# A graph kernel with four adjacency layers: masks made four blocks ahead, left-over weights made in the first sweep, and three transfer slots instead of four with one more pair of blocks kept in SBUF

## What is computed

```
layer 0: 1 - 0.1*h - 0.01*sum(h * (adj @ h))
layer 1: twice  h = tanh(concat(adj @ h, h) @ W[k])
layer 2: support = h @ weight
         rank = cumsum(adj != 0, axis=1); deg = rank[:, -1:]; k = min(deg, 100)
         w = (adj != 0) * 0.5 ** (k - (rank - (deg - k)))   where that position is > 0
         out = w @ support + bias
layer 3: tanh(concat(h, t) @ W1 + b1) @ W2 + b2 + adj @ (h @ B.T) - rowsum(adj) * (h @ B.T)
```

## Time and profile before

| what | us |
|---|---|
| median of three runs | 791.98 (788.62 to 795.04) |
| the profiled execution, its own time | 788.66 |
| its span, first to last instruction | 786.6 |

### The profile page before, as it was taken

One profiled execution on the slowest core, in us unless ns is written; L12 is line 12 of the kernel. 1 busy time (PEld: TensorE's weight loads), 2 busy tenths in 40 slices (PEclk: granted clock), 3 DMA queues, 4 the chain that ended last, 5 costly groups with the idle time before them and its releaser, 6 DMA issues.

```text
span 786.6 us, 10295 instructions
## 1 busy us (share of the span) xinstructions
PE 714.9 (91%) x3752; PEld 287.1 (36%) x3752; DVE 468.5 (60%) x789; ACT 182.8 (23%) x279; POOL 168.7 (21%) x172
## 2 busy tenths in 40 slices
PE   1999999999899999999999967888888889999997
PEld 0333333333334333344444432333333333433333
DVE  5677666767988878555566625878888831111111
ACT  2000000000001000001010015777777731111111
POOL 5011110012000000012112232343454414222231
PEclk9999999999999999999999987999999999999999
DMA  9799999999999999999999948888999979999994
GB/s 372 312 423 420 421 419 420 421 418 366 345 387 408 385 383 374 379 358 359 362 370 367 350 192 330 328 309 316 341 349 339 330 247 373 351 369 369 367 367 191
DMA packets 48659, 280.96 MB, mean 357 GB/s; under 512 B 5985, under 2 KB 15329, under 8 KB 15713
## 3 DMA queue, kind: packets, MB, share of 16 engines
q1 hardware_dynamic: 38754, 271.39, 88.6%
q10 hardware_dynamic: 9856, 8.92, 3.5%
HBM read 275.56 MB, written 4.73 MB: 356 GB/s over the span
## 4 chain that ended last, share of the span: by engine, by line
PE 51%; DMA 31%; DVE 8%; POOL 4%; issue 4%; ACT 1%; SPq 0%; ACTq 0%; DVEq 0%; POOLq 0%
PE accA L993 34%; DMA land<-adj_blocks 15%; DMA cache<-adj_blocks 8%; DMA uS<-counts 5%; PE spare L1025 4%; DMA xin<-x_rows 3%; PE accA L1036 3%; DVE uS L835 2%; PE nat L926 2%; PE tr L902 2%; POOL rstd L495 2%; PE spare L1008 1%; PE nat L922 1%; DVE uS L825 1%; PE nat L918 1%
## 5 line engine op out<-in xcount | busy, mean ns | idle before, releaser
L993 PE MATMUL accA<-land,X 128*64 128x512 f32 x1536 | 370.1, 600 | 10.7 <-DMA land<-adj_blocks 7.8
L825 DVE TENSOR_TENSOR uS<-uS,land 128x512 f32<-128x512 f32 x192 | 133.1, 693 | 65.4 <-DMA land<-adj_blocks 56.1
L993 PEld LDWEIGHTS accA<-land,X 128*64 128x64 f32 x1536 | 103.0, 137 | 187.6 <-issue 136.2
L835 DVE TENSOR_SCALAR uS<-land 128x1024 bf16<-128x1024 f32 (+1 forms) x192 | 134.2, 747 | 53.6 <-DMA land<-adj_blocks 52.6
L993 PE MATMUL accA<-cache,X 128*64 128x512 f32 x512 | 126.5, 602 | 15.2 <-DVE X L867 12.5
L502 POOL TENSOR_TENSOR hS<-tS 128x256 f32<-128x256 f32 x32 | 25.6, 802 | 475.5 <-DVE tS L706 475.5
L407 ACT ACTIVATE wS<-spare 128x1024 uint16<-128x1024 f32 x112 | 108.6, 1033 | 56.2 <-PE spare L1025 56.0
L1025 PE MATMUL spare<-uS,triA 128*128 128x512 bf16 x256 | 78.5, 389 | 30.7 <-DMA uS<-counts 11.0
L1036 PE MATMUL accA<-wS,X 128*128 128x512 bf16 x256 | 77.7, 386 | 0.0
L583 ACT ACTIVATE rowsT<-tr 128x256 f32<-128x256 f32 x40 | 15.4, 385 | 236.2 <-PE tr L902 236.2
L993 PEld LDWEIGHTS accA<-cache,X 128*64 128x64 f32 x512 | 36.6, 138 | 83.2 <-issue 76.9
(11 more groups left out here) (78 smaller groups left out, 465.8 us busy)
## 6 DMA issues: line engine op xcount, KB each, us to landing
land<-adj_blocks SPq DMA_DIRECT2D x240, 1024.0 KB, 7.6
cache<-adj_blocks SPq DMA_DIRECT2D x16, 1024.0 KB, 12.3
xin<-x_rows ACTq DMA_DIRECT2D x32, 128.0 KB, 5.5
x_rows<-zS ACTq DMA_DIRECT2D x24, 128.0 KB, 5.0
cache<-x_rows SPq DMA_DIRECT2D x1, 1024.0 KB, 4.9
loadjS<-adj_blocks SPq DMA_DIRECT2D x64, 8.0 KB
uS<-counts SPq DMA_DIRECT2D x64, 4.0 KB
out_rows<-zS ACTq DMA_DIRECT2D x8, 128.0 KB, 7.3
```

The lines of the kernel that those rows point to most:

```text
L825: nc.vector.tensor_tensor(total, total, of[:, i * W:(i + 1) * W], ALU.add)\
L835: nc.vector.tensor_scalar(masks(b)[0:rows, :], block_of(p, c, b)[0:rows, :], 0.0, None, ALU.not_equal)\
L993: last = nc.tensor.matmul(accA[k * D:(k + 1) * D, c % 2, :], tile(X[p % 2], TQ * b + k), of[:, k * W:(k + 1) * W], start=(b == 0), stop=(b ...
```

## The change

The edits, with the names of the new code:

1. `LAND` is 3. `cached_pairs(7)` is (0, 2, 4), so 17 pairs stay in SBUF and 47 are transferred in a sweep after the first.
2. In the first sweep the two pairs of chunk 1 that stay in SBUF are issued ahead of pair (0, 6) (`L0_LOADS`).
3. The left-over weights are made in L0, for each chunk: SP brings the left-over adjacency (`left_adjacency`, from an array that the host lays out), VectorE combines it with the counts, ScalarE forms the weight, and a transfer puts it in DRAM. In L2 one transfer per chunk brings it back (`left_over`). GpSimd's three operations in L2 are gone. The left-over rows are copied chunk by chunk, by four small transfers each (`left_rows_of`), at the head of the steps of L1B from chunk 2 on, and in L2.
4. In L2 the masks are made `LEAD` = 4 blocks ahead of the block to which the other work belongs; `EVAC_LAG` is 1.
5. The row sums of L1B's chunks go ahead of the `nat` matmuls, into a bank of their own use, and TensorE waits for other semaphores at the start of L2.

```diff
 def cached_pairs(c):
-    return (0, 4)
+    return (0, 2, 4) if c == 7 else (0, 4)
...
+L0_LOADS = [(c, k) for c in range(NC) for k in range(PAIRS)]
+for _k in cached_pairs(1):
+    L0_LOADS.remove((1, _k))
+    L0_LOADS.insert(L0_LOADS.index((0, 6)), (1, _k))
+
+LAND = 3
-LAND = 4
...
+LEAD = 4
-EVAC_LAG = 3
+EVAC_LAG = 1
...
-        sums_p = spare[:, 0, 0:4]
+        sums_p = nat[:, CH:CH + 4]
...
+            def left_adjacency(c):
+                if c:
+                    sp.wait_ge(left_later, c)
+                else:
+                    sp.wait_ge(cleared, 1)
+                sp.dma_start(loadjS[1:2 * NT:2, :], left_in_d[:, c * W:(c + 1) * W]).then_inc(left_adj, 16)
             def left_over(c):
-                if c:
-                    sp.wait_ge(left_ready, c)
-                rows = adj_in.rearrange("(b p) (t w) -> p b t w", p=P, t=2 * TQ)
-                for k in range(PAIRS):
-                    sp.dma_start(loadjS[4 * k:4 * k + 4, :], rows[LAST, c * PAIRS + k]).then_inc(left_in, 16)
-                sp.dma_start(locntS[:, :], tile_counts[c, :, 1]).then_inc(left_in, 16)
+                if c >= 2:
+                    sp.wait_ge(weighed, c - 1)
+                sp.dma_start(left_weights(c), left_d[c]).then_inc(left_in[c % 2], 16)
+
+            def left_rows_of(c):
+                sp.wait_ge(cleared, 1)
+                sp.wait_ge(copy_used, copied_no(L1B, c, 1) + 1)
+                for t in range(4 * c, 4 * c + 4):
+                    sp.dma_start(loS[2 * t + 1:2 * t + 2, :], tile16(t)[LAST:P, :]).then_inc(left_rows, 16)
...
-                if g == 6:
-                    sp.wait_ge(copy_used, copied_no(L1B, NC - 1, 1) + 1)
-                    sp.dma_start(left_d, X[1][LAST:P, :].bitcast(F16)).then_inc(left_rows, 16)
-                    sp.wait_ge(left_rows, 16)
-                    sp.dma_start(loS[:, :], left_d.rearrange("o (t w) -> (o t) w", w=2 * D)).then_inc(left_rows, 16)
+                if g in (2, 6):
+                    left_rows_of(NC - 2 if g == 2 else NC - 1)
...
                 if p == L2 and c == 0:
                     sp.wait_ge(counts_out, 16 * NC)
+                    sp.wait_ge(left_out, 16 * NC)
                     left_over(0)
+                    left_over(1)
                     after_masks(0)
-                for k in range(PAIRS):
+                if p == L1B and c >= 2:
+                    left_rows_of(c - 2)
+                if (p, c) == (L1A, 0):
+                    left_adjacency(NC - 1)
+                for c, k in [(c, k) for k in range(PAIRS)] if p != L0 else L0_LOADS[c * PAIRS:(c + 1) * PAIRS]:
...
+                    if p == L0 and k == 5 and c:
+                        left_adjacency(c - 1)
...
+                    nc.scalar.activation(loweightS, lolaterS, ACT.Relu, bias=wt("full", rows=(0, D)),
+                                         scale=-BIT * BIT).then_inc(left_made, 1)
+                    act.wait_ge(left_made, c + 1)
+                    act.dma_start(left_d[c], loweightS).then_inc(left_out, 16)
...
+                        dve.wait_ge(left_adj, 16 * (c + 1))
...
+                        nc.vector.scalar_tensor_tensor(out=lolaterS, in0=loadjS, scalar=0.0, in1=countS,
+                                                       op0=ALU.is_equal, op1=ALU.max).then_inc(left_later, 1)
...
+                if p == L2 and NQ * c + b + LEAD < NQ * NC:
+                    mask(p, (NQ * c + b + LEAD) // NQ, (b + LEAD) % NQ)
...
             def step(p, c, before, before2):
+                if p == L2 and c == 0:
+                    for b in range(LEAD):
+                        mask(p, c, b)
```

More of the change, by code:

```diff
@@ L913, in epilogue @@
                     nat_free(nat_no(p, c, 0))
+                    if p == L1B:
+                        pe.wait_ge(totalled, totalled_no(L1B, c, TOTALS[L1B][-1]))
+                        if c:
+                            pe.wait_ge(rowsum_ready, c)
+                        for j in range(4):
+                            last = nc.tensor.matmul(sums_p[:, j:j + 1], totals(c)[:, j * P:(j + 1) * P], wt("ones"),
+                                                    start=True, stop=True)
+                        last.then_inc(sums_done, 1)
                     if p in (L1A, L1B):
@@ L928, in epilogue @@
                     last.then_inc(nat_done, 1)
-                    if p == L1B:
-                        pe.wait_ge(totalled, totalled_no(L1B, c, TOTALS[L1B][-1]))
-                        if c:
-                            pe.wait_ge(rowsum_ready, c)
-                        for j in range(4):
-                            last = nc.tensor.matmul(sums_p[:, j:j + 1], totals(c)[:, j * P:(j + 1) * P], wt("ones"),
-                                                    start=True, stop=True)
-                        last.then_inc(sums_done, 1)
                 if at == ("transpose" if p == L3 else HT_PE.get(p, None)):
@@ L1052, in step @@
                     count(NC - 1, NQ - 1)
-                if p == L1B and c == 0:
+                if p == L2 and c == 0:
                     pe.wait_ge(count_ready, NC)
-                if p == L2 and c == 0:
-                    pe.wait_ge(rowsum_ready, NC)
                 if s >= 2:
```

84 lines of the change are left out of this document (42 added, 42 removed).

## The result

The changed kernel takes 905.4 us in the median (900.21 to 920.36, four runs), the kernel before 793.5 beside it. The ratio is 1.141, 95% interval 1.131 to 1.151. The prediction was 845, with a range of 816 to 872. The direction and the largest term were right; the size was not.

A forecast was written before the change was run, and what follows sets the result against it. It took transfers to bound L0, TensorE to bound L1A, L1B and L3, and only L2 to have room. 50.4 + 12 + 3 + 2.2 + 3 + 2.4 + 0.5 - 18.3 = 55.2 us more gave 845 us, range 816 to 872.

The forecast's parts named there:

- the largest term: SP's added wait in L1B: TensorE stalls 8.4 us in each of six chunks, 50.4 us.
- L0: start, traffic: L0: queue dry sooner at the start with three slots, 3 us; adjacency in and weights out, 2.2 us.
- L2 with its start: L2: chunks 1.9 us shorter, 13.3 us over seven, plus 5 us at its start; 18.3 us gained.
- three slots in L3: L3: loads issued one pair later cost almost nothing, as chunks are over 1 us longer; 0.5 us.
- The wait at the head of L1B's chunks: L1B, chunks 2 to 7: SP waits for GpSimd's split, holding all loads; TensorE stands 8.4 us each.
- The clock: L1B: each stall lowers TensorE's clock for the work behind it, 2.0 us a stall, 12 us for six.
- the clock stays up: Rival, L1B: stalls do not lower the clock, so 12 us less, 833 us; chance 0.12.
- Three slots: L1A, L1B, L3: loads issued one pair later still land nearly in time; 2.4, 0 and 0.5 us.
- three slots starve the sweeps: Rival: 1.3 us lost in each of 24 chunks of L0, L1A and L3, 31 us, 873 us; chance 0.06.
- The turn to L1A: L0's end: SP waits for VectorE's last work, so L1A's first loads land late; 3 us, bounds 0 and 5.
- the early loads fill no hole: L0: the two pairs moved ahead of (0, 6) stand behind (0, 5), which itself waits for a slot.
- the first half turn: L2 chunk from block 12's move to block 4's: TensorE bounds, 8.9 us; the other half, VectorE-bound, 9.4 us.

The follow-up runs named there:

- e1: The changed kernel with L1B's four left-over row copies and their wait moved behind the chunk's last load: 841.6 us, ratio 1.060 to the kernel before.
- e7: The changed kernel with ten extra unused matmuls put ahead of block 2 in L1B's chunks 2 to 7: 898.4 us, ratio 1.124 to the kernel before.
- e2: The kernel before with only SP's wait for GpSimd's split added at the head of L1B's chunks 2 to 7, no copies: 846.5 us, ratio 1.068.
- e3: The kernel before with LAND = 3 and nothing else: 839.8 us, ratio 1.060.
- e5: The changed kernel with four slots, pairs (0, 4) kept, and L1B's row copies behind the chunk's last load: 787.2 us, ratio 0.989 to the kernel before.
- e4: The changed kernel with LAND = 4 and pairs (0, 4) kept in every chunk: 867.9 us, ratio 1.094 to the kernel before.
- e13: e12 with the xin transfer in L2 issued three blocks earlier in ScalarE's program: 780.7 us, ratio 0.982 to the kernel before.
- e12: e5 with the last left-over adjacency row fetched behind L1A's load (0, 3), not at L1A's head: 787.8 us, ratio 0.988 to the kernel before.
- e8: The kernel before with only L2's masks made four blocks ahead (LEAD 4, EVAC_LAG 1): 791.9 us, ratio 0.993.

## Why the prediction was right and where it failed

In the prediction's own terms, with the span's 117.9 us set beside its 55.2. (Two slips in its sums are small: 8 chunks of 0.31 us of queue are 2.5 and not 2.2, and 843.9 with the 3.3 of the median is 847 and not 845.)

| term | predicted | measured |
|---|---|---|
| L1B: wait, clock, three slots | 50.4 + 12 + 0 = 62.4 | 84.2 |
| L0: start, traffic | 3 + 2.2 = 5.2 | 10.2 |
| turn to L1A, three slots in L1A | 3 + 2.4 = 5.4 | 20.9 |
| L2 with its start | -18.3 | -7.0 |
| three slots in L3 | 0.5 | 9.6 |

1. **The wait at the head of L1B's chunks: right.** Place, chain, number of stalls and releaser are as predicted. With the fourth slot back, moving it is worth 77.5 us of L1B. The stall was 9.4 us and not 8.4, since a small transfer's issue was 0.6 us there and not 0.34; I had taken the duration from another kind of small transfer. Of the 21.8 us by which L1B missed, 5.7 are the wait (e1 gives back 68.1 of L1B for 62.4) and 16.1 what e1's L1B is still longer than before's: the slots.

2. **The clock: right.** 2.0 us a stall was predicted; e7 gives 1.6 of time, e2 2.5 of busy time. The rival "the clock stays up" is refuted by the 0.51 above.

3. **Three slots: this is the step that failed.** It read: "The load issued at 257.08 would go out at 258.8 and, alone, land at 263.7 ... So 0.3 us for a chunk of L1A ... L1B and L3 have chunks over 1 us longer, so 0 and 0.5." It followed one load of one chunk, and took 4.9 us for it, the time of a load into idle queues. With three slots the median was 6.2, with two loads still ahead of it. The ring as a whole should have been summed: with the latency of the very row used (7.05 us) and the 1.89 us of sweep, three slots give (7.05 + 1.89)/3 = 2.98 us a pair against the 2.78 that L1A had, 48 pairs, 10 us. e3 measured 12.9. That this comes so near is partly luck: the landing fell to 6.2 with three slots, which with 1.89 gives 2.70 and no loss at all, and the time for which a slot was held was 2.9. What the sum does show is that nothing was left to spare. The bound of 12 for L1A was thus nearly right, and the value chosen below it was not. The rival "three slots starve the sweeps", at 0.06, was the case that happened, on top of the stalls. Its price of 31 us was for L0, L1A and L3, where e3 lost 22.4; one line costs 47, because L1B, which prediction and rival left out for its longer chunks, lost most, 21.5 us. The path there leads through VectorE: its row sums wait for late loads (67.6 us, 42.8 before), its layer norm stands behind them, and TensorE's transposes wait for the norm (`hS`): 12.5 us, and 6.4 for loads.

4. **The turn to L1A: the right mechanism, a size too small.** 3 us was predicted. With four slots, where the ring costs nothing, L1A of e5 is 5.3 us longer and e4's 6.9, and 4 of e5's 5.3 go away with the later fetch. TensorE's two idle times at the turn are 1.9 and 2.1 us in e5 and in the changed kernel, near the predicted 3. The rest is waits for the next loads and the clock, 2.5 us of busy time in e5, which the prediction had put at nothing here.

5. **L0: mis-sized.** The left-over work costs 6.2 to 6.6 and not 2.2, the slots 2.1 and not 3. That the early loads fill no hole fits the runs with three slots; with four they seem to be worth some us.

6. **L2: right in its parts, but taken back.** A chunk of 18.3 us was predicted; undisturbed ones took 18.5, in the changed kernel too (five of its seven took 18.5 to 18.9). I had the first half turn bounded by TensorE and the second by VectorE, with the loads hidden. But two of the seven took 22.6 and 20.8 us, late landings with three slots, and the start gave 2 us and not 5 (from L1B's last matmul to chunk 0's matmul with the left-over weights 33.6 us, 35.7 before). Hence 7.0 for 18.3; e13 has 14.0. The prediction never looked at `xin`, though VectorE waited 4.9 us for it in L2 before. That cost it nothing here, since the changed kernel does not wait for `xin` in L2; e5 and e12 do.

The miss of 62.7 us is therefore L1B 21.8, L1A 15.5, L2 11.3, L3 9.1, L0 5.0, and by the runs over half of it is the ring of three: 37.5 us between the medians of the changed kernel and e4, 47 by e3, for the 2.9 predicted (5.9 with the 3 for L0's start). The wait, undone alone in the changed kernel (e1), gives back 63.8 us.

## What to carry to other kernels

Before a buffer is taken from a ring, add up its whole turn, the median from issue to landing in this traffic plus the hold, divide by the number of buffers and compare it with the pace of the stage; if little is left, the spread of the landings is paid in full, in every stage. A wait in a queue that issues transfers holds up all that stand behind it: put it behind the loads that someone needs soon, and look up when rows "of two chunks ago" are really made. And where a stage has slow and fast turns with the same work, compare a slow one with a fast one: a small transfer beside large ones may be what is late.

## What the runs showed of the hardware

- The issue of a small transfer took 0.60 us for a row copied from SBUF (four in 2.40), and 0.34 for each of eight from DRAM. It is not the source alone: a row of counts, also from DRAM, took 0.55 (L428 of the kernel before).
- A 128 KB transfer landed 4.8 to 8.7 us after its issue in the chunks of e12's L2, where 1 MB loads were under way; the 1 MB loads there took 7.4 in the median.
- Landing times of equal loads in L1A spread from 4.8 to 9.9 us with four slots and from 4.7 to 8.3 with three. One slot less shortened the median by 1.2 us only.
- Ten 128x512 float32 matmuls (20 records) in the stall kept TensorE at 2.4 GHz: in e7 the granted clock was 1.00 over the stall and the 10 us behind it, 0.51 from 428.0 to 438.1 us in the changed kernel.
- Behind idle times of 1.9 and 2.1 us the granted clock over the first chunk of L1A was 0.93 in e5; in the kernel before, with 0.3 us there, it was 1.00.
- A VectorE mask of 127x1024 took 0.85 us in the mean beside GpSimd's work on 32x512 tiles (e8) and 0.71 without it (e5).
